# Cross attention: stacked rows three partitions apart in runs of 8 KB, and the odd heads' stacks issued by GpSimd

## The reference

```
h = layernorm(x)
q = (h @ Wq + bq) -> 16 heads of 16;  k = (ctx @ Wk + bk);  v = (ctx @ Wv + bv)
scores = q . k * scale           # per batch and head, 256 x 256
x = x + (softmax(scores) @ v) @ Wo + bo
```

## Time and profile before

| | us |
|---|---|
| median of three runs | 2549.36 |
| lowest, highest | 2547.86, 2559.96 |
| profiled execution | 2551.32 |
| its span on the core | 2549.6 |
| PE busy | 2233.4 (88%) |
| DVE busy | 1249.1 (49%) |
| ACT busy | 1044.1 (41%) |
| POOL busy | 690.6 (27%) |
| mean granted TensorE clock | 0.945 |

### The profile page before, as it was taken

The page is one execution under the profiler, slowest core; times in us unless marked ns, Lnnn a source line. Parts: engine busy times, 40 slices in busy tenths (PEclk is TensorE's granted clock), DMA queues, the critical chain, the costliest instruction groups (busy, mean ns, idle before and its releaser), DMA issues. The chain is left out here.

```text
span 2549.6 us, 43063 instructions
## 1 busy us (share of the span) xinstructions
PE 2233.4 (88%) x13610; PEld 1651.1 (65%) x13611; DVE 1249.1 (49%) x2762; ACT 1044.1 (41%) x2555; POOL 690.6 (27%) x684
## 2 busy tenths in 40 slices
PE   8998398668898999898898998999997599879998
PEld 4664398434465874466785664679996356558887
DVE  4664300379776229876434664100000466567864
ACT  1664133213565433466532663134443046544332
POOL 1000200337522436621541000320001410044443
PEclk8999699789999999999998998999998789999999
DMA  7761143110000000000007741133221476100001
GB/s 183 160 168 69 49 166 111 40 42 0 26 0 15 26 17 0 25 0 4 11 10 143 126 78 73 40 116 106 72 105 51 102 154 125 33 26 20 25 26 34
DMA packets 110836, 164.30 MB, mean 64 GB/s; under 512 B 15272, under 2 KB 95256, under 8 KB 105720
## 3 DMA queue, kind: packets, MB, share of 16 engines
q1 hardware_dynamic: 101712, 140.68, 21.6%
q0 software_dynamic: 7680, 20.98, 2.7%
q10 hardware_dynamic: 1320, 1.03, 0.2%
HBM read 114.96 MB, written 47.32 MB: 64 GB/s over the span
## 5 line engine op out<-in xcount | busy, mean ns | idle before, releaser
L1037 DVE TENSOR_REDUCE xa_mx<-ps 128x2 f32<-128x512 f32 x384 | 247.0, 686 | 103.0 <-PE ps L689 101.8
L141 PE MATMUL ps<-ones 128*128 128x384 f32 (+1 forms) x450 | 165.1, 496 | 100.9 <-DMA ex_rows<-rows_out,rows_back 39.0
L896 ACT ACTIVATE xn_tok<-ps 128x512 f32<-128x512 f32 x384 | 210.6, 602 | 52.2 <-PE ps L697 50.3
L1476 PEld LDWEIGHTS ps<-ex_xT,ex_w 128*128 128x128 f32 x1792 | 210.7, 194 | 7.3 <-issue 4.5
L1476 PE MATMUL ps<-ex_xT,ex_w 128*128 128x128 f32 x1792 | 211.3, 277 | 3.9 <-issue 3.9
L1483 PE MATMUL ps<-ex_w,ex_h 128*128 128x256 f32 x896 | 202.7, 379 | 0.0
L141 PEld LDWEIGHTS ps<-ones 128*128 128x128 f32 x450 | 90.8, 223 | 145.6 <-issue 52.1
L689 PE MATMUL ps<-xa_ks,xa_qs 48*128 48x256 f32 (+1 forms) x768 | 158.8, 328 | 27.4 <-DMA xa_qs<-x_queries 9.4
L2141 PE MATMUL ps<-lo_w,lp_hs 128*128 128x512 f32 x384 | 176.1, 610 | 4.8 <-ACT lp_hs L2189 2.8
L1483 PEld LDWEIGHTS ps<-ex_w,ex_h 128*128 128x128 f32 x896 | 166.1, 190 | 20.0
L689 PEld LDWEIGHTS ps<-xa_ks,xa_qs 48*128 48x128 f32 (+1 forms) x768 | 107.8, 197 | 101.7 <-DVE xa_mx L1037 53.0
(11 more groups left out here) (344 smaller groups left out, 5006.6 us busy)
## 6 DMA issues: line engine op xcount, KB each, us to landing
xa_ks<-x_keys SPq DMA_DIRECT2D x144, 128.0 KB
xa_qs<-x_queries SPq DMA_DIRECT2D x144, 128.0 KB, 4.3
ex_w<-in_L0f_w_dram SPq DMA_DIRECT2D x16, 1024.0 KB, 7.1
ex_w<-in_L2f_w_dram SPq DMA_DIRECT2D x16, 1024.0 KB, 6.9
x_keys<-xa_khl SPq DMA_DIRECT2D x24, 512.0 KB, 5.3
x_queries<-xa_qhl SPq DMA_DIRECT2D x24, 512.0 KB, 3.0
ex_stage<-rows_in POOLq DMA_DIRECT2D x64, 128.0 KB, 2.3
rows_out<-ex_rows SPq DMA_DIRECT2D x56, 128.0 KB, 1.7
```

What stands on the lines that cost most here:

```text
L141: self.nc.tensor.matmul(self.ps[:, bank, 0:wide * P], self.ones[:], self.ones[:].unsqueeze(1).to_broadcast([P, wide, P]), start=True, stop ...
L896: nc.scalar.activation(pT[:, h % SLOTS].rearrange("p k q -> p (k q)"), c.ps[:, S_BANK + (HEADS * b + n) % 3], ACT.Exp).then_inc(exped.sem, 1)
L1037: nc.vector.tensor_reduce(mx[:, half, :, col], c.ps[:, M_BANK + h % 2].rearrange("p (t n) -> p t n", t=2), AX_X, ALU.max).then_inc(max_put ...
L1476: ins = nc.tensor.matmul(c.ps[:, f % 4, 0:P], w1[:, buf, k, f * P:(f + 1) * P], xT[:, k], start=(k == 0), stop=(k == KD - 1))
```

## The change

The columns of Wq and Wk (and bq, bk) are reordered when the inputs are laid out, so that a projected channel stands at parity, row within the head, pair (`j r g`) and no longer at pair, parity, row (`g j r`). In DRAM the eight heads of one row are then adjacent: each partition's load is one run of 8 KB. The three copies of a row go to adjacent partitions (`at = 64 * j + n`, then every third partition), for keys and for queries alike. The stack functions take the issuing engine and the parity: SP issues those of j = 0, POOL those of j = 1. PE waits for both; each parity has its own semaphores. The bytes and the number of DMAs stay as they are.

```diff
-    K_LOADS = 6 + 2 * masked
+    K_LOADS, Q_LOADS = 3 + masked, 3
...
+        def stack_keys(eng, j, b):
+            eng.wait_ge(*k_sent(16 * b + 16))
+            if b >= K_BUFS:
+                eng.wait_ge(*scored_T(HEADS * (b - K_BUFS + 1)))
+            parts = dram["x_keys"][b].rearrange("(a j r g) t -> a j r g t", a=2, g=PAIRS, j=2)
+            for n, part in enumerate((0, 0, 1)):
+                at = 64 * j + n
+                eng.dma_start(ks[at:at + 3 * HD - 2:3, b % K_BUFS].bitcast(F32), parts[part, j]
+                              ).then_inc(k_in[j][b % 3].sem, 16)
+            if masked:
+                at = 64 * j + 3 * HD
+                eng.dma_start(ks[at:at + 1, b % K_BUFS].bitcast(F32), ...)
...
+        def stack_queries(eng, j, b):       # the same way, parts (0, 1, 0)
...
         @block.gpsimd
         def _(pool):
...
             for n, (lo, hi) in enumerate(GROUPS):
                 pool.wait_ge(*variance(n + 1))
                 nc.gpsimd.tensor_tensor(rstd[:, lo:hi], var[:, lo:hi], c.half[:, 1, lo:hi], ALU.pow
                                         ).then_inc(powered.sem, 1)
+            if masked:
+                pool.wait_ge(*rows_masked(2))
+            for b in range(B):
+                if b == 0:
+                    stack_keys(pool, 1, 0)
+                    stack_queries(pool, 1, 0)
+                    stack_keys(pool, 1, 1)
+                    stack_queries(pool, 1, 1)
+                    stack_keys(pool, 1, 2)
+                if biased:
+                    add_bias(b)
+                if b + 2 < B:
+                    stack_queries(pool, 1, b + 2)
+                if b + 3 < B:
+                    stack_keys(pool, 1, b + 3)
...
-            stack_keys(0)
-            stack_queries(0)
+            stack_keys(sp, 0, 0)
+            stack_queries(sp, 0, 0)
...
                         if n == 0:
-                            pe.wait_ge(*k_in[(b + 1) % 3](16 * K_LOADS * ((b + 1) // 3 + 1)))
-                            pe.wait_ge(*q_in[(b + 1) % 2](16 * 6 * ((b + 1) // 2 + 1)))
+                            for j in range(2):
+                                pe.wait_ge(*k_in[j][(b + 1) % 3](16 * K_LOADS * ((b + 1) // 3 + 1)))
+                                pe.wait_ge(*q_in[j][(b + 1) % 2](16 * Q_LOADS * ((b + 1) // 2 + 1)))
```

More of the change, by code:

```diff
@@ L68 @@
 rows_sent scratch_zeroed even_part_in odd_part_in tile_stored quarter0_back quarter1_back quarter2_back
-quarter3_back output_weights_in local_weights_in affine_in keys_sent queries_sent rows_set key_weights_in query_weights_in mask_in first_context_in context_in first_x_in x_in ident_in first_keys_in second_keys_in third_keys_in even_queries_in odd_queries_in lower_max_in
+quarter3_back output_weights_in local_weights_in affine_in keys_sent queries_sent rows_set key_weights_in query_weights_in mask_in first_context_in context_in first_x_in x_in ident_in first_keys_in second_keys_in third_keys_in even_queries_in odd_queries_in first_upper_keys_in second_upper_keys_in third_upper_keys_in even_upper_queries_in odd_upper_queries_in lower_max_in
 upper_max_in lower_max_sent upper_max_sent router_in tile_in""".split()
@@ L473, in xattn_phase @@
     k_sent, q_sent, rows_set = c.sig("keys_sent"), c.sig("queries_sent"), c.sig("rows_set")
-    k_in = [c.sig("first_keys_in"), c.sig("second_keys_in"), c.sig("third_keys_in")]
-    q_in = [c.sig("even_queries_in"), c.sig("odd_queries_in")]
+    k_in = [[c.sig(n + part + "keys_in") for n in ("first_", "second_", "third_")] for part in ("", "upper_")]
+    q_in = [[c.sig(n + part + "queries_in") for n in ("even_", "odd_")] for part in ("", "upper_")]
     max_sent = [c.sig("lower_max_sent"), c.sig("upper_max_sent")]
@@ L518, in xattn_phase @@
         S_BANK, M_BANK, O_BANK, Y_BANK, W_BANK = 0, 3, 5, 6, 7
+        def stack_keys(eng, j, b):
[9 more added lines that the diff above has]
+                at = 64 * j + 3 * HD
+                eng.dma_start(ks[at:at + 1, b % K_BUFS].bitcast(F32),
+                              mbias[:, b * S:(b + 1) * S].bitcast(F32).unsqueeze(1).to_broadcast([1, PAIRS, S])
+                              ).then_inc(k_in[j][b % 3].sem, 16)
+        def stack_queries(eng, j, b):
+            eng.wait_ge(*q_sent(16 * b + 16))
+            if b >= Q_BUFS:
+                eng.wait_ge(*scored_T(HEADS * (b - Q_BUFS + 1)))
+            parts = dram["x_queries"][b].rearrange("(a j r g) t -> a j r g t", a=2, g=PAIRS, j=2)
+            for n, part in enumerate((0, 1, 0)):
+                at = 64 * j + n
+                eng.dma_start(qs[at:at + 3 * HD - 2:3, b % Q_BUFS].bitcast(F32), parts[part, j]
+                              ).then_inc(q_in[j][b % 2].sem, 16)
         @block.gpsimd
@@ L538, in _, with add_bias @@
                                         ).then_inc(powered.sem, 1)
-            if biased:
[L540 to L544, removed]
+            def add_bias(b):
+                if b == 0:
+                    pool.wait_ge(*loaded(16 * n_loads))
+                pool.wait_ge(*normed(b + 1))
+                xb = c.x[:, 2 * b:2 * b + 2]
+                nc.gpsimd.tensor_tensor(xb, xb, bo[:].to_broadcast([P, 2, D]), ALU.add).then_inc(bias_added.sem, 1)
+            if masked:
+                pool.wait_ge(*rows_masked(2))
+            for b in range(B):
+                if b == 0:
+                    stack_keys(pool, 1, 0)
[9 more added lines that the diff above has]
+                    stack_keys(pool, 1, b + 3)
+            if biased:
                 pool.wait_ge(*bias_added(B))
@@ L580, in send_queries @@
                              qhl[:].bitcast(F32).rearrange("p a c t -> p (a c) t")).then_inc(q_sent.sem, 16)
[L582 to L607, removed]
             send_keys(0)
@@ L620, in _ @@
             send_queries(1)
-            stack_keys(1)
-            stack_queries(1)
+            stack_keys(sp, 0, 1)
+            stack_queries(sp, 0, 1)
             send_keys(2)
-            stack_keys(2)
+            stack_keys(sp, 0, 2)
             if masked:
@@ L630, in _ @@
                     send_queries(b + 2)
-                    stack_queries(b + 2)
+                    stack_queries(sp, 0, b + 2)
                 if b + 3 < B:
                     send_keys(b + 3)
-                    stack_keys(b + 3)
+                    stack_keys(sp, 0, b + 3)
                 if masked:
@@ L1121, in xattn_phase @@
     for n in range(3):
-        k_in[n].spent(16 * K_LOADS * len(range(n, B, 3)))
+        for j in range(2):
+            k_in[j][n].spent(16 * K_LOADS * len(range(n, B, 3)))
     for par in range(2):
-        q_in[par].spent(16 * 6 * (B // 2))
+        for j in range(2):
+            q_in[j][par].spent(16 * Q_LOADS * (B // 2))
         max_sent[par].spent(16 * B)
@@ L2860, in _layouts, with by_row @@
     o["ctxT"][KC[1], 1] = 1.0
+    def by_row(w):
+        return w.reshape(w.shape[:-1] + (HEADS // 2, 2, HD)).swapaxes(-3, -2).swapaxes(-2, -1).reshape(w.shape)
     for tag, src in (("L0x_", "L0_xattn_"), ("L2x_", "L2_xattn_"), ("L3x_", "L3_xattn_")):
         for name in ("Wq", "Wk", "Wv", "Wo"):
-            o[tag + name.lower()] = _chunked(a[src + name])
-    o["L2x_wk"][KC[1], 1] = a["L2_xattn_bk"]
+            w = a[src + name]
+            o[tag + name.lower()] = _chunked(by_row(w) if name in ("Wq", "Wk") else w)
+    o["L2x_wk"][KC[1], 1] = by_row(a["L2_xattn_bk"])
     o["L2x_wv"][KC[1], 1] = a["L2_xattn_bv"]
-    o["L2x_qcol"] = a["L2_xattn_bq"].reshape(KD, P).T
+    o["L2x_qcol"] = by_row(a["L2_xattn_bq"]).reshape(KD, P).T
     o["L2x_bo"], o["L3x_bo"] = a["L2_xattn_bo"].reshape(1, 1, D), a["L3_xattn_bo"].reshape(1, 1, D)
```

## The result

The changed kernel takes 2562.3 us (median of 11 runs, 2557.5 to 2573.2) against 2552.3 us for the kernel before on the same chip (11 runs): a ratio of 1.0048, 95% interval 1.0029 to 1.0066 (the quotient of the two medians is 1.0039; the ratios here are those on record, which differ from such quotients by up to 0.1%). It is slower, by an amount close to the 0.5% that the prediction took as the least that can be told from no change. The forecast was 2555 with a range of 2543 to 2568.

The account below looks back on a forecast made before the run. The prediction took PE to bound the main loops, with stack loads mostly hidden. Its terms, 13.5 - 2.5 - 5.5 = +5.5 us on the profiled 2551.3, gave 2556.8, or 2555 us in the runs' terms, range 2543 to 2568.

Parts of the forecast that it names:

- The start of a phase: First scores in L0, L2 and L3 come later, as POOL's stacks wait behind the second pow: +13.5 us, ends +4.9 and +24.1.
- the stretch after it: After each phase's first score, waits for first maxima and batch 2's rows mostly vanish: -2.5 us, ends 0 and -2.7.
- the main loops: Cheaper stacks give back half of the waits for maxima and the clock loss after them: -5.5 us, ends 0 and -10.9.
- The steps: At a phase's start, POOL issues one stack every 0.70 us, after a gap of 0.3 us behind the pow.
- The landing: At a phase's start, POOL's last stack lands 2.6 us after its issue: 2.3, and 0.3 for writing onto 16 partitions.
- SP's shorter list: At a phase's start, SP has six issues instead of twelve, which only brings batch 1 in earlier.
- The clock costs no more: At a phase's start, the clock is already at 0.50 after 2.85 us of waiting; longer waits can't lower it further.
- 7.5 us and what follows them: In the main loops, all that can return: 7.5 us of PE's waits for maxima, plus at most 3.4 us of clock.
- The statement on the rows' places: For stack loads, old and new rows load ports equally over three stacks, some 160 GB/s; both halves together give up to twice.
- the traffic doesn't shrink: Rival: full DMA engines gain little from a second queue or longer runs, loops give back nothing; +12.5, 2562 us, chance 0.18.
- POOL's issue is dear: Rival: POOL needs 1.25 us per stack issue, so the phases' starts cost 24.1 us; +16, 2565 us, chance 0.17.
- The maxima win: Rival: all waits for maxima and the clock's 3.4 us return, POOL issues as fast as SP; -8.7, 2541 us, chance 0.15.

Follow-up runs that it names:

- e1: The changed kernel with POOL issuing its stacks of batch 0 ahead of the second pow instead of behind it; 2526.4 us, 0.9898 of the kernel before.
- e5: The changed kernel with SP's stacks of batch 1 held until POOL's queries of batch 0 have landed; 2556.5 us, 1.0018 of the kernel before.
- e9: The changed kernel plus measuring SP loads in eleven partition patterns at the end of L3's cross attention; its total says nothing, only the loads' GB/s count.
- e3: The kernel before (old rows, 1 KB pieces) with the odd heads' stacks issued by POOL in the changed kernel's places; 2568.0 us, 1.0076.
- e4: The kernel before with runs of 8 KB, still on neighbouring partitions and every stack issued by SP; 2555.9 us, 1.0026.
- e2: The changed kernel's new rows and 8 KB runs, but every stack issued by SP in the old order; 2528.4 us, 0.9915 of the kernel before.
- e6: The kernel before with rows on every third partition, still 1 KB pieces and all stacks by SP; 2534.0 us, 0.9932.
- e8: The kernel before with later batches' stack loads moving one of eight heads' rows, scores made from stale rows; 2540.8 us, 0.9953.

## Why the prediction came out as it did

**The number** came nearer than its parts. On the profiled executions +5.5 us was forecast and +6.2 measured, but the start missed by +8.2, the stretch after it by -5.0, the main loops by -4.6 and the untouched stages by +2.1, and these nearly cancel: that is luck. In the runs' terms the forecast also stood on a median of three runs, 2549.4, where eleven gave 2552.3; the medians moved by 10.0 us.

**The start of a phase** was the right step and decides the sign, as e1 against the changed kernel shows (0.9898 against 1.0048, with only these issues moved). Its size was +21.7 where +13.5 was forecast, inside the ends of 4.9 and 24.1. By terms:
- The steps were dear in the forecast: 0.70 each and a gap of 0.3. POOL issued its stacks every 0.48 to 0.58 us with no gap, so from the pow's end to the last issue's beginning it took 3.2 us in L0 and 2.5 in L2 and L3, against 4.5, 3.8 and 3.8: -3.8 in all. L0's pow itself ended 1.3 us earlier than in the earlier trace rows.
- The landing was the mis-sized term: 2.6 us forecast, 7.3, 7.1 and 7.0 measured, +13.6. It was taken from loads of 128 KB with little beside them, but here a load lands behind what stands ahead of it or flows beside it: six stacks of POOL's own batch 0 and six of SP's batch 1 are 1.57 MB, 8.0 us at 197 GB/s. The kernel before already showed it: the stacked queries' own landings (the line below) have a median of 4.3 us and reach 9.5; the 2.3 of the earlier trace rows is that of POOL's expert loads, and the 0.3 added to it stands in no row. The prediction counted SP's shorter list as help; in fact it moved batch 1 onto batch 0. e5 takes SP's part away and gets back 6.3 us of waiting.
- Together -3.8 - 1.3 + 13.6 = +8.5, the difference between 21.7 and 13.5 within 0.3.

```profile
DMA to landing us min/median/max: 2.7/4.3/9.5
```

**"The clock costs no more"** held, and more than that: after the longer wait the clock was at its upper level when the loops began (the windows at 61 to 69 above: 0.62 before, 1.00 after). In the stretch from first score to main loop this and the quieter queue gave back 7.5 us where 2.5 were forecast; in e9's execution of the same code it was 2.5, so the term's size is not settled.

**The main loops** gave back 10.1 us (5.0, 3.2 and 2.0, the first only just within the 5 us each beyond which the prediction called itself wrong), the forecast 5.5 with an end of 10.9. Of the waits for maxima only 2.5 us came back, so the term "7.5 us and what follows them" is not how it came: more of it goes with the clock. Summed over windows of 2 us, the time that the loops spent at the clock's lower level went from 34.0 us before to 12.7 after, in e3, with the old rows, to 16.0; at half the clock that is worth half as much work, 17.0, 6.4 and 8.0 us. e3's loops are 7.8 us shorter than those of before although its waits for maxima are the same 7.4. In e4, with the old rows and an early start, it was 39 us, in e1, e2 and e6, with the new rows and an early start, 22 to 25. So a part of what the changed kernel seems to win in its loops goes with a start that waits longer, and it is paid for there; no run varies the wait alone. The traffic itself is worth some 12 us at most (e8), and it is won cleanly in e2.

**The statement on the rows' places** was wrong in what it was used for. "The spacing by itself gives little and running both halves at once gives up to twice" is the other way round in the times: spacing alone 0.9932 (e6), the second queue alone 1.0076 (e3), and with spacing in place the second queue adds nothing that these runs can tell (e1 and e2 overlap). In the rates neither is so: while only stacks flow, the old rows moved 131 to 136 GB/s on one queue (e4 and before) and 147 to 163 on two (e3), the new ones 152 to 161 on one (e6 and e2) and 197 to 216 on two. Spacing or the second queue alone gives some 15%, both together half as much again, and nothing gave twice. The table was right, as e9 shows, but it was used for three loads added together, where old and new rows come out alike, at an estimated 160 GB/s: the new rows reach that, the old ones do not. One load of the old rows has four rows on each of four ports, and moves 116 GB/s if nothing else flows; one of the new has one to three on each of eight. That engines which finish a lightly loaded port early go on to the next stack would explain why three apart does better in the kernels than its 137 GB/s alone; no run shows which engine does what, and this stays an explanation. The other rate that the prediction leaned on, "a load onto 128 partitions 363 GB/s", was also a mixed window: from 40 to 47 us the context's load (packets of 6 KB) was followed by the two stores of batch 1 (packets of 1 KB). Loads onto 128 partitions alone moved 401 (e9).

**The rivals.** The time fits the rival "the traffic doesn't shrink" (2562 us), its mechanism does not: the stacks went from 136 to 197 GB/s and the share in L3's loop from 0.48 to 0.38. The Trainium skill's rule (DMA: Bandwidth & Descriptors, "Rules for kernel authors") that several issuing engines add no bandwidth does not agree with these traces, and the measurement decides: two queues moved 147 to 163 GB/s for 131 to 136 and 197 to 216 for 152 to 161. In time it comes to the same, as two queues with the old rows left the maxima's waits at 7.4 us (e3) and with the new rows won nothing clear (e1 against e2). "POOL's issue is dear" is refuted by 0.48 to 0.58 us a step. "The maxima win" would have been decided by cheap issues; they were cheap and the landing ate them.

**What stays open.** Why executions of one kernel differ by some 10 us. e5's profiled one took 2545.9 with a median of 2556.5, and its main loops 482.1 us, wholly at the clock's upper level, where the changed kernel's took 490.7 and 491.1 in two executions; so e5's loops say nothing certain about its edit. Also open is whether two apart for two of the three parts would beat three apart; no run tried it.

## What to carry to other kernels

Before moving DMAs to another engine's queue, look at what that engine is waiting for at the moment at which they are due, and count everything that will be in flight when they land; a landing time taken from a quiet stretch is a lower end. A DMA share near 1 does not say that the bytes move as fast as they can: compare the GB/s, over windows many packets long, with those of other loads at the same share, and if a load touches few partitions, spread its rows. When a layout and a queue are changed at once, run each alone: here the layout was the gain and the queue's place in the order was the loss.

## What the runs showed of the hardware that was not expected

- Sixteen partitions take 116 GB/s when they are neighbours and 193 to 203 when they stand 2, 4, 5 or 8 apart, but 137 at 3 apart; 32 and 64 neighbours 200 and 203, 128 neighbours 401 (e9), all at a share of 0.86 to 0.99.
- Loads onto different halves from two queues moved 197 to 216 GB/s where one queue moved 152 to 161 (changed kernel against e2 and e6), and 147 to 163 where one moved 131 to 136 (e3 against e4 and before).
- For loads onto 16 partitions, runs of 8 KB and of 1 KB made no difference: 131 and 136 GB/s on neighbours (e4 and before).
- SP's issue of a stack took 431 ns before, 420 in e4, 589 in the changed kernel and 600 in e6: the spaced destination costs it some 0.17 us. POOL's took 494 ns spaced and 530 with the old rows (medians).
